# Value projections laid between the first maxima of attention, operands loaded during the adapter, and the last group's units exchanged

## The chip, the core and the metric

The program runs on one core of a Trainium2 chip. The core has five engines that run their own instruction lists and wait for each other with semaphores: TensorE (PE, matrix products; PEld is its loading of weights), VectorE (DVE), ScalarE (ACT), GpSimd (POOL) and SyncE (SP, which here only issues transfers). Matrix products go to PSUM, a memory of eight banks of 128 partitions x 512 floats; everything else lies in SBUF. The metric is the device time of one execution in microseconds; lower is better. One execution was also profiled, and all rows below come from it.

## What is computed

Two transformer layers in a row over 1024 tokens of 512 channels. The part that the change touches is the attention of both layers:

```python
# layer 0 (32 heads of 16 channels, causal), and an adapter of 10 prefix tokens
q, k, v = split(x @ w_attn.T); q, k = rope(q), rope(k)
y  = softmax(mask(q @ k.T / sqrt(16))) @ v
y += gating * softmax(q @ ak.T / sqrt(512)) @ av     # ak, av: projections of adapter_wte
x  = layernorm(x + y @ w_proj.T)
...
x  = layernorm(x + lookup(x))                        # memory lookup, not touched
# layer 1: 32 query heads share 8 key/value heads
q, k, v = x @ Wq, x @ Wk, x @ Wv; ... same attention, no adapter
x  = layernorm(x + y @ Wo)
x  = layernorm(x + swiglu(x))                        # not touched
```

## The kernel before, in words

`load_and_project` makes q and k of a layer in units of 128 channels x 512 tokens, rotates them, cuts each value into three bf16 parts that sum to it, and stores the parts in DRAM (`q_parts`, `k_parts`). Products with x and w are done as three fp32r products of cut operands (`products`, one output tile is 12 matmuls of 512 columns). In layer 1 this phase also makes the values v, as the last thing on PE: two tiles of 12 matmuls, copied by ACT into `v_T`, turned on PE in eight transposes and copied by ACT into `v_tok`.

`adapter` (layer 0 only) follows. Its list `order` sets what PE and ACT do: scores of four token tiles, then softmax of that half on DVE and ACT (`prob`), then for each of eight token tiles n a turn ("T": four transposes, ACT copies to `pT`) and a product ("y", ACT copies to `ad["y"]`). Between them stand eight tiles of the value projection ("V", 12 matmuls each, one ACT copy to `v_tok`). SP waits for the last V before it loads the first stacked operands of attention (`load_first`), because `arena_s`, where they go, also held the cut weights `w0_hl`.

`attention` works in units `(c, g)`: g is one of 8 groups of 4 heads, c one of 2 blocks of 512 query tokens. Unit c=0 is short (4 key tiles), c=1 long (8 key tiles). There are 16 units, c inside g. For each unit three things happen:

- *maxima*: bf16 products of q and k with a causal mask (lines 861 and 866), reduced by DVE (line 1001), joined by DVE (976), split by POOL (`split_max`, lines 1024 to 1030), turned on PE (entry "T", line 850), copied by DVE (992), and sent by an ACT-issued transfer into the rows under q (`load_max`, line 958). They run ahead of the unit by `LEAD` columns in three PSUM banks (`RING`).
- *scores* (line 886), exponentials on ACT (947), triangular masks on POOL for the diagonal tiles (1052).
- *values* (line 904), and one ACT copy of the unit's result (954, `copy_o`).

Before the first scores PE issues `maxima(0, 0)`: 48 entries, that is all maxima of units 0 and 1, the first of unit 2 and the turns of both units. This stretch is called the ramp below. `issued_by(u, slot)` tells how many entries PE has issued by a slot of unit u; POOL and ACT place their own work by it:

```python
while split < NU and min(first_entry[split + 1] + 3, first_entry[NU]) \
        <= issued_by(u, max(0, 2 * b - 4)):
    split_max(split)
```

ACT calls `load_max(u + 1)` at its fifth pair of exponentials of unit u. POOL starts the phase with three memsets (`k_st[KS:KM]`, line 1033) and `load_v(0)` (line 1010). Phases end with a barrier of all engines.

Of the kernel before, what the change touches and what calls it, by code (L numbers as in the profile page):

```python
# [26 lines left out]
F32 = mybir.dt.float32  # L27
# [80 lines left out]
def build(nc, d, out):  # L108
    with ExitStack() as stack:
# [5 lines left out]
        def at(name, offset, shape, dtype=F32):  # L115
# [22 lines left out]
        w0_hl = [at(f"w0_{n}", M_S + 24576 * n, [P, KC, 3 * C], F32R) for n in range(2)]  # L138
# [49 lines left out]
            w_hl=w0_hl, x_hl=x0_hl, q_parts=q_parts[0], k_parts=k_parts[0], ones=ones, eps=eps,  # L188
# [9 lines left out]
        adapter(nc, d, ad, x_loaded, x_tok, v_tok, w0_hl, x0_hl, arena_o, ident, gating, psum, stacked,  # L198
                wo[0], wo_hl[0])
        attention(nc, 0, att, stacked, arena_o, arena_p, arena_x, v_tok, v_grp, ident_b, maskb, psum,  # L200
                  (x_tok[:, :, :], d["x"].rearrange("(t p) c -> p t c", p=P), x_loaded))
# [15 lines left out]
        attention(nc, 1, att, stacked, arena_o, arena_p, arena_x, v_tok, v_grp, ident_b, maskb, psum)  # L217
# [45 lines left out]
def load_and_project(nc, d, layer, m):  # L263
# [8 lines left out]
    v_T = view(m["arena_w"], 0, [CH, 512])  # L272
# [28 lines left out]
    def cut_of(piece):  # L301

        kind, k, n0 = piece
        return [a[:, k, n0:n0 + 512] for a in ((x_raw, xh, xl) if kind == "x" else (w, wh, wl))]
# [8 lines left out]
    with Phase(nc, f"proj{layer}") as ph:  # L313
# [7 lines left out]
        v_ready, v_copied, consts = ph.sem("v_ready"), ph.sem("v_copied"), ph.sem("consts")  # L321
# [55 lines left out]
        def _(pe):  # L377
# [23 lines left out]
            if layer == 0:  # L401
# [12 lines left out]
                return  # L414

            for c in range(CH):
                products(pe, psum[:, 4 + c, :],
                         [lambda k, a=a: a[:, k, C + nk * P:n_out] for a in (wh, wl)],
                         [lambda k, a=a: a[:, k, 512 * c:512 * c + 512] for a in (xh, xl)])\
                    .then_inc(v_ready, 1)  # L420
            for c in range(CH):
                pe.wait_ge(v_copied, c + 1)
                for t in range(4):
                    last = pe.transpose(psum[:, 6 + c, P * t:P * t + P],
                                        v_T[:, c, P * t:P * t + P], m["ident"][:, :])
                last.then_inc(v_ready, 1)

        @block.scalar
        def _(act):
# [26 lines left out]
            for c in range(CH if layer == 1 else 0):  # L456
                act.wait_ge(v_ready, c + 1)
                act.copy(v_T[:, c, :], psum[:, 4 + c, :]).then_inc(v_copied, 1)
            for c in range(CH if layer == 1 else 0):
                act.wait_ge(v_ready, CH + c + 1)  # L460
                act.copy(v_tok[:, 4 * c:4 * c + 4, 0:P],
                         psum[:, 6 + c, :].rearrange("p (t f) -> p t f", f=P)).then_inc(v_copied, 1)
# [83 lines left out]
def adapter(nc, d, ad, x_loaded, x_tok, v_tok, w_hl, x_hl, arena_o, ident, gating, psum, stacked,  # L546
# [22 lines left out]
    turns = [what for what in order if what[0] in "VT"]  # L569
# [4 lines left out]
    with Phase(nc, "adapter") as ph:  # L574
# [19 lines left out]
        def _(pe):  # L594
            for what, n in order:
                if what == "scores":
# [22 lines left out]
                if what == "V":  # L619
                    last = products(pe, psum[:, bank, :],  # L620
                                    [lambda k, a=a: a[:, k, P * n:P * n + P] for a in x_hl],
                                    [lambda k, a=a: a[:, k, 2 * C:3 * C] for a in w_hl])
                else:
                    pe.wait_ge(prob_ready, n // HT + 1)
                    for t in range(KC):
                        last = pe.transpose(psum[0:AW, bank, P * t:P * t + P],
                                            prob[n // HT][:, n % HT, AW * t:AW * t + AW], ident[:, :])
# [3 lines left out]
        def _(act):  # L631
            for what, n in order:
# [3 lines left out]
                if what in "VT":  # L636
                    turn = turns.index((what, n))
                    bank = 4 + turn % 2
                    act.wait_ge(turn_ready, turn + 1)
                    if what == "V":  # L640
                        act.copy(v_tok[:, n, :], psum[:, bank, :]).then_inc(turn_taken, 1)
                    else:
                        if n >= 2:
                            act.wait_ge(y_ready, n - 1)
                        act.copy(pT[:, n % 2, :, :], psum[0:AW, bank, :].rearrange(
                            "p (t q) -> p t q", q=P)).then_inc(turn_taken, 1)
                if what == "V" and n in (0, 2):
                    half = n // 2
                    act.wait_ge(shifted, half + 1)
                    act.activation(prob[half], prob[half], ACT.Exp, scale=float(C) ** -0.5)\  # L650
                        .then_inc(exped, 1)
# [84 lines left out]
def attention(nc, layer, phase, stacked, arena_o, arena_p, arena_x, v_tok, v_grp, ident_b, maskb,  # L736
# [64 lines left out]
    with phase as ph, ExitStack() as own:  # L801
# [39 lines left out]
        def _(pe):  # L841
# [30 lines left out]
            def scores(u, kt, p):  # L872
# [4 lines left out]
                if kt == 0 and p == 0:  # L877
                    pe.wait_ge(max_loaded[u % NS], 16 * (u // NS + 1))
                    if u == 0:
                        pe.wait_ge(rows, NK)  # L880
# [936 lines left out]
```

## Time and profile before

| what | us |
|---|---|
| median of 3 runs (range) | 1014.57 (1011.73 to 1017.09) |
| the profiled execution: its time | 1011.6 |
| its span in the trace | 1009.9 |
| PE / DVE / ACT / POOL busy | 915.9 / 669.6 / 503.5 / 278.4 |
| adapter, from PE's first to the barrier behind it | 96.4 to 138.2 |
| ramp of layer 0, to its last turn | 138.3 to 165.1 |
| ramp of layer 1, to its last turn | 567.3 to 592.9 |

The span is what the trace covers; the 1.7 us between it and the time lie around the program and are taken as fixed. PE is the busiest engine by far, so the table is read by stages: in some of them PE sets the pace, in others it is paced by another.

### The profile page before, as it was taken

To read this page: it belongs to the slowest core of one execution; us is meant where nothing else is said; L and a number is where in the kernel's file an instruction comes from. 1 tells how busy PE (TensorE), PEld (TensorE's weight loads), DVE (VectorE), ACT (ScalarE), POOL (GpSimd) and SP (SyncE) were. 2 spreads that over 40 slices of the span, in tenths; PEclk is the share of its full clock that TensorE was granted. 3 is DMA by queue.
4 is the path that set the end of the run, shared out by engine and by line. 5 is a ranking of instruction groups with operands and counts; after the bars stand their busy time and mean duration, and the time that the engine had idled before them with its cause. 6 is when DMAs were issued, how large, how long until landed. Compare 5 with 4: busy or idle time off the path is not lost. (4 is left out here: it accounts for less than half of the span.)

```text
span 1009.9 us, 15158 instructions
## 1 busy us (share of the span) xinstructions
PE 915.9 (91%) x5334; PEld 503.2 (50%) x5334; DVE 669.6 (66%) x1177; ACT 503.5 (50%) x1134; POOL 278.4 (28%) x527
## 2 busy tenths in 40 slices
PE   6887989999999998988698599999999889799997
PEld 4555853433444432855365233434444338577766
DVE  5975547877788760965748577877778518455464
ACT  5221322776766665224612146777767652367630
POOL 2454141223223321033345122223223212013200
PEclk9997985999999999988789779999999999899999
DMA  9332060221212110200023400111100010321001
GB/s 323 94 95 79 1 149 25 55 53 54 65 49 63 47 40 7 99 1 1 0 75 112 111 22 25 37 40 39 41 26 2 2 42 1 136 82 64 22 32 53
DMA packets 50029, 57.14 MB, mean 57 GB/s; under 512 B 8928, under 2 KB 39712, under 8 KB 49952
## 3 DMA queue, kind: packets, MB, share of 16 engines
q1 hardware_dynamic: 48320, 55.75, 18.4%
q8 instruction: 45, 0.74, 0.3%
q10 hardware_dynamic: 1632, 0.39, 0.2%
q14 instruction: 32, 0.26, 0.1%
HBM read 43.41 MB, written 12.32 MB: 55 GB/s over the span
## 5 line engine op out<-in xcount | busy, mean ns | idle before, releaser
L1001 DVE TENSOR_REDUCE mx<-psum 128x1 f32<-128x512 f32 (+3 forms) x640 | 370.6, 631 | 114.5 <-PE psum L866 70.1
L861 PE MATMUL psum<-arena_s 96*128 96x512 bf16 (+3 forms) x768 | 226.5, 349 | 9.6 <-DVE mx L1001 5.5
L947 ACT ACTIVATE arena_p<-psum 128x512 f32<-128x512 f32 (+1 forms) x384 | 185.1, 591 | 92.7 <-PE psum L886 61.6
L886 PE MATMUL psum<-arena_s 99*128 99x512 bf16 (+3 forms) x768 | 204.4, 335 | 8.5 <-ACT arena_p L947 3.3
L947 ACT ACTIVATE arena_x<-psum 128x128 f32<-128x128 f32 (+2 forms) x384 | 133.9, 439 | 88.6 <-PE psum L886 65.7
L861 PEld LDWEIGHTS psum<-arena_s 96*128 96x128 bf16 x768 | 71.2, 99 | 124.4 <-DVE mx L1001 70.9
L886 PEld LDWEIGHTS psum<-arena_s 99*128 99x128 bf16 x768 | 66.9, 98 | 100.9 <-ACT arena_p L947 34.4
L1052 POOL TENSOR_SCALAR_AFFINE_SELECT arena_p<-arena_p 128x256 f32<-128x256 f32 x128 | 50.9, 408 | 204.2 <-ACT arena_p L947 204.2
L259 PE MATMUL psum<-x_h,w 128*128 128x512 f32 x224 | 87.9, 456 | 10.8 <-DVE w L476 7.6
L866 PE MATMUL psum<-maskb,ident_b 128*128 128x128 bf16 (+1 forms) x384 | 96.5, 251 | 0.0
L904 PE MATMUL psum<-arena_p,v_grp 128*32 128x512 f32 (+1 forms) x768 | 91.5, 597 | 0.0
L1052 POOL TENSOR_SCALAR_AFFINE_SELECT arena_x<-arena_x 128x256 f32<-128x256 f32 x128 | 51.4, 408 | 76.9 <-ACT arena_x L947 47.2
L904 PE MATMUL psum<-arena_x,v_grp 128*32 128x256 f32 (+2 forms) x768 | 59.0, 421 | 4.6 <-POOL arena_x L1052 4.6
L434 ACT CAST arena_p<-arena_o 128x512 bf16<-128x512 f32 x26 | 16.1, 619 | 87.3 <-DMA q_parts<-arena_p 42.7
L259 PEld LDWEIGHTS psum<-x_h,w 128*128 128x128 f32 x224 | 44.8, 200 | 27.5 <-DVE w L476 9.2
L1603 PE MATMUL psum<-x_h,ff_w 128*128 128x512 f32 (+1 forms) x176 | 45.7, 403 | 1.6 <-ACT ff_flags L1660 0.9
L468 DVE CAST arena_p<-arena_o 128x512 bf16<-128x512 f32 x26 | 32.2, 1240 | 21.6 <-POOL arena_o L542 21.5
L259 PE MATMUL psum<-x_l,w 128*128 128x512 f32 x112 | 46.2, 413 | 0.0
L1603 PE MATMUL psum<-x_l,ff_w 128*128 128x512 f32 (+1 forms) x176 | 45.2, 399 | 0.0
L1140 PE MATMUL psum<-wo_h,yT 128*128 128x512 f32 x128 | 43.8, 403 | 1.6 <-DVE arena_s L1213 1.6
L542 POOL TENSOR_TENSOR arena_o<-arena_o,arena_p 128x512 f32<-128x512 f32 x26 | 31.7, 1220 | 46.5 <-ACT arena_p L434 46.5
L538 POOL TENSOR_TENSOR arena_o<-arena_o 128x512 f32<-128x512 f32 x26 | 34.3, 1319 | 33.2 <-DVE arena_o L494 33.2
(202 smaller groups left out, 1203.6 us busy)
## 6 DMA issues: line engine op xcount, KB each, us to landing
q_parts<-arena_p SPq DMA_DIRECT2D x48, 128.0 KB
arena_s<-q_parts SPq DMA_DIRECT2D x32, 192.0 KB, 2.9
arena_s<-k_parts SPq DMA_DIRECT2D x96, 64.0 KB, 2.3
ff_raw<-in_w_in SPq DMA_DIRECT2D x11, 512.0 KB, 3.6
arena_s<-q_parts SPq DMA_DIRECT2D x32, 128.0 KB, 3.0
k_parts<-arena_p SPq DMA_DIRECT2D x30, 128.0 KB
arena_w<-in_w SPq DMA_DIRECT2D x12, 256.0 KB, 6.5
ff_wd_raw<-in_w_down SPq DMA_DIRECT2D x1, 2560.0 KB, 11.3
```

The source lines that it names most:

```text
L259: last = pe.matmul(out, lhs[i](k), rhs[j](k), start=k + n == 0, stop=k == KC - 1 and n == 2)
L468: dve.tensor_copy(parts[:, n % 2, 1, :], t_cos[:, n % 2, :]).then_inc(mid_ready, 1)
L538: pool.tensor_tensor(rotated(n), t_cos[:, s, :], t_sin[:, s, :], ALU.add)\
L861: last = pe.matmul(psum[:, bank, width * n:width * n + width], q_st[0:KS, b % NS, 512 * r + P * i:512 * r + P * i + P], k_st[0:KS, g % NK, ...
L866: last = pe.matmul(psum[:, bank, 0:width * n].rearrange("p (h k) -> p h k", h=n) [:, :, width - P:width], ident_b[:, :], maskb[:, :].rearr ...
L886: pe.matmul(psum[:, 2 * (n % 2) + t, o:512], k_st[0:KM, g % NK, at:at + P], q_st[0:KM, u % NS, 512 * r + o:512 * r + 512], start=True, sto ...
L904: last = pe.matmul(psum[32 * r:32 * r + VW, 6, o:512], v_grp[:, u // CH % 2, kt, r if layer == 0 else 0, :], pr[(n + r // 2) % NP_RING][:, ...
L947: act.activation(pr[n % NP_RING][:, t, o:512], psum[:, 2 * (n % 2) + t, o:512], ACT.Exp, scale=scale).then_inc(exp_ready, 1)
L1001: dve.tensor_reduce(mx[:, b % 2, kc, col:col + 4 * len(heads) - 3:4], src, AX, ALU.max)\
L1052: pool.affine_select(out=tri, in_=tri, compare_op=ALU.is_ge, fill=0.0, base=0, pattern=[[0, 2], [1, P]], channel_multiplier=-1).then_inc(m ...
L1140: last = pe.matmul(psum[:, 5, :], yT_hl[i][:, t % 2, k, :], w_out[j][:, k, :], start=k + n == 0, stop=k == KC - 1 and n == 2)
L1603: last = pe.matmul(psum[0:rows[i], 2 * (n % 3) + u, :], ff.w_hl[a][:, i % 2, col:col + rows[i]], x_hl[b][:, k, 512 * c:512 * c + 512], sta ...
```

## The change

Five edits. (1) In layer 0 the 96 value matmuls leave the adapter, in layer 1 the 24 value matmuls and eight transposes leave the projection phase; both are laid between the entries of the ramp (`v_product`, `v_turn`): by entry e of 48, e/42 of them are issued. ACT's copies of them come at the head of its list in attention. (2) The cut weights of v get arrays of their own (`wv0_hl`) at the end of the old ones, so SP issues `load_first` at the adapter's start; the loads whose place they still hold wait for the last v product. (3) POOL's memsets write 2048 floats instead of 4096 bf16, and the third one and `load_v(0)` come after the splits of units 0 and 1. (4) ACT's `load_max` is placed by `issued_by`, and slots below zero now reach back into the unit before. (5) The last two units are exchanged: (1, 7), then (0, 7).

```diff
+UNITS = [(c, g) for g in range(NG - 1) for c in range(CH)] + [(1, NG - 1), (0, NG - 1)]
...
-    order = [("scores", 0), ("V", 0), ("V", 1), ("scores", 1)]
-    for n in range(NT):
-        order.append(("T", n))
-        if n < 3:
-            order += [("V", 2 * n + 2), ("V", 2 * n + 3), ("y", n)]
-        elif n > 3:
-            order.append(("y", n - 1))
+    order = [("scores", 0), ("scores", 1)]
+    for n in range(NT):
+        order.append(("T", n))
+        if n == 2:
+            order.append(("exp", 1))
+        if n:
+            order.append(("y", n - 1))
...
-            sp.wait_ge(turn_ready, turns.index(("V", NT - 1)) + 1)
             stacked.load_first(sp)
...
+            if layer == 0:
+                stacked.load_q(sp, 3)
+            sp.wait_ge(v_ready, V_DONE)
+            if layer == 1:
+                stacked.load_q(sp, 3)
             stacked.load_q(sp, 4)
...
+                    if u == 0:
+                        pe.wait_ge(v_copied, V_COPIED)
...
-            maxima(0, 0)
+            ramp = issued_by(0, 0)
+            n_products = 3 * KC * V_DONE
+            for e in range(ramp):
+                b = next(x for x in range(NU + 1) if issued < first_entry[x + 1])
+                entry(issued, b, lists[b][issued - first_entry[b]])
+                issued += 1
+                done = min(n_products, n_products * e // (ramp - 6))
+                for i in range(done, min(n_products, n_products * (e + 1) // (ramp - 6))):
+                    v_product(i)
+                if layer == 1 and e in (ramp - 4, ramp - 1):
+                    v_turn(0 if e == ramp - 4 else 1)
...
-            load_max(0)
+            for t in range(V_DONE):
+                act.wait_ge(v_ready, t + 1)
...
+                if t == V_DONE // 2:
+                    load_max(0)
+            sent = 1
             for u in range(NU):
                 for b in range(2 * n_tiles[steps[u][0]]):
+                    while sent < NU and turn_entry(sent) < issued_by(u, 2 * b - 6):
+                        load_max(sent)
+                        sent += 1
                     exp(u, b)
                     if u and b == 3:
                         copy_o(u - 1)
-                    if u + 1 < NU and b == 4:
-                        load_max(u + 1)
```

PE's list at the start of layer 0's ramp (`arena_s` holds the stacked q and k, `maskb` the mask; line 861 before is line 847 after, 866 is 852), before:

```order
L861 MATMUL psum<-arena_s 128x128 [waits att0_k_loaded00,att0_q_loaded0]
L861 MATMUL psum<-arena_s 128x128
L866 MATMUL psum<-maskb,ident_b 128x256
L861 MATMUL psum<-arena_s 128x128 x2
L866 MATMUL psum<-maskb,ident_b 128x256
```

and after, where `wv_0` and `wv_1` are the cut weights of v and `x_h`, `x_l` the cut tokens:

```order
L847 MATMUL psum<-arena_s 128x128 [waits att0_k_loaded00,att0_q_loaded0]
L847 MATMUL psum<-arena_s 128x128
L852 MATMUL psum<-maskb,ident_b 128x256
L919 MATMUL psum<-wv_0_65,x_h 128x512
L919 MATMUL psum<-wv_1_66,x_h 128x512
L847 MATMUL psum<-arena_s 128x128 x2
L852 MATMUL psum<-maskb,ident_b 128x256
L919 MATMUL psum<-wv_0_65,x_l 128x512
L919 MATMUL psum<-wv_0_65,x_h 128x512
```

Behind each of the first 42 entries two or three value matmuls of 512 columns now stand.

ACT's list at the start of attention in layer 1 (`mT` is the turned maxima, `arena_w` holds `v_T`), before:

```order
L958 DMA arena_s<-mT 3x16x128 [waits att1_qk_taken]
L947 ACT_TABLE_LOAD
L947 ACTIVATE arena_p<-psum 128x512 [waits att1_scores_ready] x4
L947 ACTIVATE arena_p<-psum 128x384 [waits att1_scores_ready] x4
L947 ACTIVATE arena_x<-psum 128x256 [waits att1_scores_ready] x2
L958 DMA arena_s<-mT 3x16x128 [waits att1_qk_taken]
```

and after:

```order
L988 COPY arena_w<-psum 128x512 [waits att1_v_ready] x2
L980 DMA arena_s<-mT 3x16x128 [waits att1_qk_taken]
L994 COPY v_tok<-psum 128x4x128 [waits att1_v_ready] x2
L980 DMA arena_s<-mT 3x16x128 [waits att1_qk_taken]
L969 ACT_TABLE_LOAD
L969 ACTIVATE arena_p<-psum 128x512 [waits att1_scores_ready] x4
```

The second copy of turned values, the second transfer of maxima and the load of the exponential's table now stand ahead of the first exponential.

PE's list at the end of layer 1's ramp, after (line 835 is the turn of the maxima, 927 the turn of the values, 874 the scores):

```order
L847 MATMUL psum<-arena_s 128x384 [waits att1_qk_taken]
L852 MATMUL psum<-maskb,ident_b 128x128
L835 MATMUL psum<-ident_b,mst 48x128 [waits att1_max_ready,att1_qk_taken]
L927 MATMUL psum<-ident,arena_w 128x128 [waits att1_v_copied]
L927 MATMUL psum<-ident,arena_w 128x128 x3
L874 MATMUL psum<-arena_s 128x512 [waits att1_rows,att1_v_copied,att1_max_loaded0]
```

Before, the scores followed the turn of the maxima directly; now four transposes and a wait for ACT's last copy stand between.

## Rows read from the trace of the kernel before

**Rows 1.** The page's first part: busy time, share, instructions

```profile
PE 915.9 (91%) x5334; PEld 503.2 (50%) x5334; DVE 669.6 (66%) x1177; ACT 503.5 (50%) x1134; POOL 278.4 (28%) x527
```

**Rows 2.** Stretches: length, engines' busy time (PE, PEld, DVE, ACT, POOL), clock, DMA

```profile
78.00:82.00 4.00, 0.97 (x3) 0.30 (x2) 3.45 (x4) 1.10 (x2) 2.22 (x3) 1.00 0.30 96
82.00:93.00 11.00, 11.00 (x39) 8.08 (x38) 6.74 (x8) 1.24 (x2) 5.12 (x5) 0.53 0.33 106
96.40:138.30 41.90, 40.48 (x256) 35.98 (x256) 14.40 (x12) 15.68 (x26) 7.55 (x9) 1.00 0.15 37
138.30:165.10 26.80, 23.23 (x90) 7.81 (x90) 24.39 (x47) 0.00 (x0) 12.48 (x12) 0.61 0.35 84
165.10:174.90 9.80, 9.80 (x41) 3.21 (x41) 3.35 (x7) 5.15 (x14) 2.84 (x7) 0.50 0.22 62
200.00:350.00 150.00, 147.69 (x1124) 61.15 (x1121) 120.47 (x223) 104.68 (x259) 44.74 (x130) 1.00 0.21 55
545.00:549.00 4.00, 0.97 (x3) 0.19 (x2) 3.42 (x4) 1.10 (x2) 2.22 (x3) 1.00 0.29 96
567.30:592.90 25.60, 23.62 (x89) 8.43 (x89) 24.48 (x47) 1.28 (x1) 4.62 (x12) 0.63 0.25 67
```

**Rows 3.** Timeline of the adapter, DVE and ACT: start, length, engine, line

```profile
100.27 1.49 DVE L663 TENSOR_REDUCE arena_f<-psum 128x128 f32<-128x1280 f32 x1 [4.43 <-PE psum L602]
...
113.23 1.28 ACT L650 ACTIVATE arena_o<-arena_o 128x1280 f32<-128x1280 f32 x1
...
117.37 1.49 DVE L671 TENSOR_TENSOR arena_o<-arena_o,arena_f 128x1280 f32<-128x1280 f32 x1
...
130.50 1.07 ACT L645 COPY arena_o<-psum 80x512 f32<-80x512 f32 x2
...
137.30 0.59 ACT L635 COPY arena_w<-psum 128x512 f32<-128x512 f32 x1 [0.40 <-PE psum L611]
```

**Rows 4.** Timeline of PE: first matmul of value tile 1, first after it

```profile
102.88 0.61 PE L259 MATMUL psum<-w,x_h 128*128 128x512 f32 x2
...
105.60 0.56 PE L602 MATMUL psum<-arena_f,arena_o 128*128 128x80 f32 x4
```

**Rows 5.** Timeline of layer 0's ramp, POOL and PE

```profile
138.16 10.41 POOL L1033 MEMSET arena_s<- 3x4096 bf16 x3 [33.99 <-POOLq L244]
...
150.38 0.27 PE L850 MATMUL psum<-ident_b,mst 128*48 128x128 bf16 x1 [2.03 <-POOL mst L1030]
...
165.05 0.30 PE L850 MATMUL psum<-ident_b,mst 128*48 128x128 bf16 x1
```

**Rows 6.** Timeline of PE: from bf16 to fp32 operands

```profile
210.96 0.38 PE L861 MATMUL psum<-arena_s 96*128 96x512 bf16 x1
...
211.27 1.92 PE L904 MATMUL psum<-arena_p,v_grp 128*32 128x512 f32 x16
```

**Rows 7.** Timeline of ACT: first exponentials and first result copy, both layers

```profile
165.93 3.60 ACT L947 ACTIVATE arena_p<-psum 128x512 f32<-128x512 f32 x8 [28.04 <-DVE mx L1001]
...
179.87 0.59 ACT L954 COPY arena_o<-psum 128x512 f32<-128x512 f32 x1
...
593.82 3.60 ACT L947 ACTIVATE arena_p<-psum 128x512 f32<-128x512 f32 x8 [12.66 <-PE psum L886]
...
605.40 0.59 ACT L954 COPY arena_o<-psum 128x512 f32<-128x512 f32 x1
```

**Rows 8.** Timeline of layer 1: table load, last turn, sending of maxima

```profile
579.88 1.28 ACT L947 ACT_TABLE_LOAD   x1 [14.56 <-DVE mx L1001]
...
592.94 0.30 PE L850 MATMUL psum<-ident_b,mst 128*48 128x128 bf16 x1
...
597.03 0.73 ACTq L958 DMA_DIRECT2D arena_s<-mT  x1
```

**Rows 9.** Timeline of SP: last stores of layer 1's projection phase

```profile
556.29 10.19 SPq L363 DMA_DIRECT2D q_parts<-arena_p  x9
```

**Rows 10.** Timeline of ACT in layer 0's last short unit

```profile
381.39 0.45 ACT L947 ACTIVATE arena_x<-psum 128x128 f32<-128x128 f32 x2 [2.91 <-PE psum L886]
```

More of the change, by code:

```diff
@@ L595, in _ @@
             for what, n in order:
+                if what == "exp":
+                    continue
                 if what == "scores":
@@ L618, in _ @@
                 bank = 4 + turn % 2
[L619 to L627, printed above, removed]
+                pe.wait_ge(prob_ready, n // HT + 1)
+                for t in range(KC):
+                    last = pe.transpose(psum[0:AW, bank, P * t:P * t + P],
+                                        prob[n // HT][:, n % HT, AW * t:AW * t + AW], ident[:, :])
                 last.then_inc(turn_ready, 1)
@@ L635, in _ @@
                     act.copy(y_ad[:, n, :], psum[:, 6 + n % 2, :]).then_inc(y_copied, 1)
[L636 to L650, printed above, removed]
+                if what == "T":
+                    act.wait_ge(turn_ready, n + 1)
+                    if n >= 2:
+                        act.wait_ge(y_ready, n - 1)
+                    act.copy(pT[:, n % 2, :, :], psum[0:AW, 4 + n % 2, :].rearrange(
+                        "p (t q) -> p t q", q=P)).then_inc(turn_taken, 1)
+                if (what, n) in (("scores", 0), ("exp", 1)):
+                    act.wait_ge(shifted, n + 1)
+                    act.activation(prob[n], prob[n], ACT.Exp, scale=float(C) ** -0.5)\
                         .then_inc(exped, 1)
@@ L749, in attention @@
     n_tiles = [4 * (c + 1) for c in range(CH)]
-    steps = [(c, g) for g in range(NG) for c in range(CH)]
+    steps = UNITS
     NU = len(steps)
@@ L787, in issued_by @@
     def issued_by(u, slot):
-        done = sum(unit_columns[0:u]) + unit_columns[u] * slot // (4 * n_tiles[steps[u][0]])
+        if slot < 0 and u > 0:
+            return issued_by(u - 1, slot + 4 * n_tiles[steps[u - 1][0]])
+        done = sum(unit_columns[0:u]) + unit_columns[u] * max(0, slot) // (4 * n_tiles[steps[u][0]])
         return sum(1 for n in reached if n <= done + LEAD)
@@ L917, in maxima, with v_product, v_turn @@
                     issued += 1
-            maxima(0, 0)
+            def v_product(i):
+                tile, step = divmod(i, 3 * KC)
+                k, n = divmod(step, 3)
+                a, b = ((0, 0), (0, 1), (1, 0))[n]
+                xs, ws = v_from["x"], v_from["w"]
+                if layer == 0:
+                    bank, lhs, rhs = tile % 4, xs[a][:, k, P * tile:P * tile + P], ws[b][:, k, :]
+                    if step == 0 and tile >= 4:
+                        pe.wait_ge(v_copied, tile - 3)
+                else:
+                    bank, lhs, rhs = tile, ws[a][:, k, C + P:C + 2 * P], xs[b][:, k, 512 * tile:512 * tile + 512]
+                last = pe.matmul(psum[:, bank, :], lhs, rhs, start=step == 0, stop=step == 3 * KC - 1)
+                if step == 3 * KC - 1:
+                    last.then_inc(v_ready, 1)
+            def v_turn(c):
+                pe.wait_ge(v_copied, c + 1)
+                for t in range(4):
+                    last = pe.transpose(psum[:, 2 + c, P * t:P * t + P],
+                                        v_from["v_T"][:, c, P * t:P * t + P], v_from["ident"][:, :])
+                last.then_inc(v_ready, 1)
+            ramp = issued_by(0, 0)
[9 more added lines that the diff above has]
+                    v_turn(0 if e == ramp - 4 else 1)
             for u, kt in blocks[0:2]:
@@ L1030, in split_max, with minus @@
                 pool.tensor_tensor(low, md[:, :], mid, ALU.subtract).then_inc(max_ready, 1)
-            for s in range(NK):
-                pool.memset(k_st[KS:KM, s, :], -1.0).then_inc(rows, 1)
-            pool.wait_ge(rows, NK)
-            load_v(0)
+            two_minus = float(np.uint32(0xBF80BF80).view(np.float32))
+            def minus(slot):
+                pool.memset(k_st[KS:KM, slot, :].bitcast(F32), two_minus).then_inc(rows, 1)
+                pool.wait_ge(rows, slot + 1)
+            minus(0)
+            minus(1)
             split = 0
```

81 lines of the change are left out of this document (42 added, 39 removed).

## The prediction

> **What bounds the kernel now.** I read the page's first part, then a table of stretches, then the timelines of the places that the change touches. PE is busy for 91% of the span [rows 1], so the first question is where it isn't the engine that sets the pace. The stretches say so [rows 2]. In the middle of attention (200 to 350) PE is busy 147.7 of 150 us at a clock of 1.00 (2.4 GHz): work moved there would only lengthen it. In the adapter (96.4 to 138.3) PE is busy 40.5 of 41.9 us, but about half of that is the value projection. In the ramp of layer 0 (138.3 to 165.1) DVE is busy 24.4 of 26.8 us, and PE's 23.2 us of busy time stand at a clock of 0.61: it streams few columns and is paced by DVE. The ramp of layer 1 is the same picture, DVE 24.5 of 25.6 us. So the change takes work from a stretch that PE bounds and gives it to one that DVE bounds. What counts is whether the receiver has room.
>
> **Adapter, layer 0.** Without V, what is left is a chain of DVE and ACT and its tail. DVE starts on the first scores at 100.27 and ends the second half's softmax at 117.37 + 1.49 = 118.86 [rows 3]. V hardly delayed that chain: ACT's second exponential (113.23) stood behind a copy of a value tile, and by my walk through the new order it comes 0.5 us sooner, so the softmax ends at 118.4. Then four rounds of turn and product follow. In the old trace the last five turns' copies start with the pair at 130.50 (its second, the first of the second half, at 130.50 + 1.07 - 0.58 = 131.0), and the last copy ends at 137.30 + 0.59 = 137.9 [rows 3]: 6.9 us. With the same tail behind a first copy at 119.1 the adapter ends at 126.0, **-11.9 us**. V's own 96 matmuls would be more: tile 1 takes 105.60 - 102.88 = 2.72 us for 12, or 0.227 us each [rows 4], 21.8 us in all; some 10 us of it was already behind the softmax.
>
> **Loads during the adapter.** SP now issues the first operands at 96.4. The ramp's first matmul came with the barrier, before too; nothing waited for them: **0**. They are hidden by the softmax, and would cost at most the few us that they take to issue if that cover were gone. The loads that must wait for the last v product (third k slot, fifth q slot) are used a group later, over 20 us on.
>
> **Ramp, layer 0.** The maxima of the 48 entries are 20,736 columns of scores and 5,376 of mask (5,120 in the short unit 0, 13,312 in the long unit 1, 2,304 of unit 2; 128 columns of mask for each of 42 diagonal tiles): 26,112 columns, 10.9 us at 2.4 GHz, and with 14 ns for the start of each of some 90 instructions (what 0.227 us has over 512 columns) 12.1 us. V adds 21.8 us. That is 33.9 us of PE against DVE's 24.4: **PE becomes the bound of the ramp**. To this comes a change of operands from bf16 to fp32r and back behind each of 42 entries, which no trace of before shows. The nearest row is the step from maxima to values: a 512-column matmul starts at 210.96, the next at 211.27 [rows 6], 0.31 us where 0.22 would do, so up to 0.1 us one way. Bounds: nothing, and 0.2 us for there and back (8.4 us); I take 0.08 us, 3.4 us, nearer to the row's one way, since the trace's values also use a narrow column position. Last, the turn of unit 1 waits for DVE and POOL some 0.3 us. Together 37.5 us against 165.05 - 138.3 = 26.8 [rows 5]: **+10.7 us**. PE's wait of 2.03 us for POOL behind 10.41 us of memsets [rows 5] goes too, but it was DVE's slack and is inside this difference.
>
> The Trainium skill (TensorE: Matmul & The Clock Gate, LDWEIGHTS) has a load of weights take its columns over 1.2 GHz, which for 128 columns is an estimated 107 ns, about 53 ns more than the 128-column mask ahead of it covers. By that rule the 42 changes would cost at most 2.3 us, and the whole sum below would be about 1 us less; no run here shows it.
>
> **First exponentials, layer 0.** ACT now sends the maxima of unit 1 before its first exponential. It waits for DVE's copy of the last turn and then issues for 0.73 us [rows 8]: an estimated **+0.9 us**. Against it stands the clock: from 165.1 to 174.9 PE ran at 0.50 [rows 2]. From first exponential to first result copy layer 0 took 179.87 - 165.93 = 13.9 us, layer 1, mostly at 2.4 GHz, 605.40 - 593.82 = 11.6 us [rows 7]. A ramp full of products should leave the clock high: **-2.4 us**. `load_v(0)` and the third memset (about 0.6 and, by half of 3.47 us a memset, 1.8 us) are covered by ACT's first pair of exponentials.
>
> **Layer 1.** The end of the projection phase is set by SP: nine stores issued from 556.29 for 10.19 us, to 566.48 [rows 9], less than 1 us before the ramp. They wait for the parts of the last two units, not for PE's value products. Taking these away gives **0**. In the ramp 24 products (5.5 us) and eight transposes (some 1.1 us: four of them are at most 0.6 of a round's 1.4 us in the adapter's tail, 6.9 us over five) join 12.1 us of maxima: 19 us, within DVE's 24.5, so they are hidden at 2.4 GHz. At 1.2 GHz, as in much of this ramp (clock 0.63 in rows 2), they aren't: each entry with its half product then takes PE 860 columns or 0.72 us against DVE's 24.4 / 46 = 0.53, until the clock comes back. For some seven entries that is **+1.3 us** (bounds 0 and, at 1.2 GHz throughout, 8). The end of the ramp is surer. Before, the last turn was at 592.94 and the first exponential at 593.82, 0.9 us [rows 7, 8]. Now four transposes (0.6 us with the start), ACT's copy (0.6), the issue of the second maxima (0.73) and the table load of 1.28 us, which had been done idle at 579.88 [rows 8], stand in line: 3.6 us, **+2.8 us** (bounds 2 and 3.5).
>
> **The exchanged units.** The tail without maxima has the same columns either way. PE's wait for POOL's last mask ahead of unit 14 stays, since POOL still splits the last maxima ahead of that mask, and DVE is done with them no sooner. The wait of ACT for 2.91 us came with a low clock [rows 10]. I take **0**, bounds -4 and +2 a layer. The new places of `load_max` and of the splits move nothing that PE waited for in the middle: **0**.
>
> **The clock in the adapter.** Without V, PE idles in it three times: about 3 us while DVE takes the first scores, 2 us, and 3.9 us ahead of the fifth turn. Two similar stretches with PE busy 0.97 of 4 us stand in rows 2: after 78 to 82 the clock was 0.53 for 11 us, in 545 to 549 it stayed 1.00. At 1.2 GHz a round of the tail takes PE about 2.9 us instead of 1.4, over four rounds 6 us. I take half: **+3.0 us**.
>
> **Sum.** -11.9 + 3.0 + 10.7 + 0.9 - 2.4 + 1.3 + 2.8 = **+4.4 us**. The profiled execution took 1011.6 us (span 1009.9 and 1.7 around it), so it would take 1016.0. The median of the runs lies 3.0 above it; against that the forecast is 1014.6 + 4.4 = **1019.0 us**, +0.4%. About 0.5% (5 us) is what a measurement of this kernel can tell from no change.
>
> **The rivals.**
> - *The clock falls early and stays down (slower).* If PE is at 1.2 GHz from the first gap to the start of the ramp, the second scores take 3.7 us more, the tail 6 instead of 3, and the ramp, now bound by PE, loses 2.5 us or more until the clock is back; with as much again in layer 1's ramp the sum is about +14, 1028 us. It decides from 1 us of extra low time on the PE-bound part. For it: after 82 the clock stayed low for 11 us of busy PE. Against it: the second gap in rows 2. The Trainium skill (TensorE: Matmul & The Clock Gate, Why this matters for your kernels) tells to leave no long idle gaps between bursts, since the clock then falls to half; it speaks for this rival, and the trace agrees once and disagrees once. Chance 0.25.
> - *The tail gains and the gaps are harmless (faster).* If the long unit ahead of the short one keeps PE fed, its low clock and ACT's wait of 2.91 us go, about 4 us in layer 0 and 3 in layer 1. With a full clock in the adapter (-3) the sum is about -5.5, 1009 us. Against it: the wait for the mask, which begins it, stays. Chance 0.16.
> - *The change does what it says: V is hidden in DVE's ramp.* Then the ramp stays 26.8 us and the sum is -6.3, 1008 us. Against it stand 75,000 columns, 31 us at 2.4 GHz, in a ramp of 27. Only a wrong count of mine would allow it. Chance 0.09.
> - *Forecast.* Chance 0.50, own range 1014 to 1024.
>
> **How the numbers follow.** The range of 0.8 runs from the faster cases (1008) to the better part of the slow one (1027). Faster by over 0.5% (under 1009.5) holds most of the two faster cases, 0.19. Slower (over 1019.6) holds nearly all of the slow clock and 0.16 of the forecast, 0.40. Within 0.5%: 0.41.
>
> **What the new profile would show.** The adapter should be 29 to 33 us long with PE's clock below 1 in its last third; the ramp of layer 0 37 to 38 us with PE busy throughout at clock 1.00, DVE waiting between reductions, and no wait for the memset; the first exponential of layer 1 about 3.6 us behind the last turn, with the table load right ahead of it; layer 1's projection phase still ending with some 10 us of stores on SP; both tails 29 to 31 us. A ramp of layer 0 under 34 us, or a tail under 27, would make me wrong to the fast side; a ramp over 40 us, or a clock of 0.5 in it, to the slow side.

## The result, and the profile after

The changed kernel takes 1061.26 us (median of 4 runs, 1059.92 to 1063.06) against 1014.21 us for the kernel before: a ratio of 1.046, 95% interval 1.043 to 1.050. It is 47 us slower; the prediction said 4.4 us slower, with a range up to 1027.

The first thing to do with a miss of this size is to find the stretch. ACT copies each unit's result once, so its copies (line 954 before, 976 after) are milestones in both traces. From the starts of the first and the last copy of each layer:

| stretch | before, us | after, us | difference | the prediction's sum |
|---|---|---|---|---|
| to the first copy of layer 0 | 179.87 | 184.29 | +4.4 | +0.3 |
| first to last copy, layer 0 | 220.02 | 237.63 | +17.6 | 0 |
| to the first copy of layer 1 | 205.51 | 209.68 | +4.2 | +4.1 |
| first to last copy, layer 1 | 221.54 | 241.72 | +20.2 | 0 |
| to the end of the span | 182.94 | 184.88 | +1.9 | 0 |

So 37.8 of the 48.3 us by which the span grew were lost in the middle of attention, where the prediction had put nothing. The first part of the profile's page has PE's share down from 91% [rows 1] to 88%, with the same number of matmuls in it:

```profile
PE 929.9 (88%) x5334; PEld 510.8 (48%) x5334; DVE 672.7 (64%) x1177; ACT 502.8 (48%) x1134; POOL 272.9 (26%) x527
```

The view of stretches shows where (columns: stretch, its length, busy time of PE, PEld, DVE, ACT and POOL, PE's clock, DMA):

```profile
core 0: us, PE busy (x) PEld busy (x) DVE busy (x) ACT busy (x) POOL busy (x), PEclk, DMA share, GB/s
200.00:350.00 150.00, 138.31 (x1014) 55.68 (x1012) 108.17 (x200) 94.00 (x231) 39.69 (x118) 0.98 0.20 52
```

PE was busy for 147.7 of these 150 us before [rows 2]; now it stands for 11.7. The groups of PE's lines in the same stretch name what it waits for (line 874 is the scores):

```profile
L847 PE MATMUL psum<-arena_s 96*128 96x512 bf16 (+3 forms) x222 | 60.8, 327 | 1.0 <-DVE mx L1036 1.0
L874 PE MATMUL psum<-arena_s 99*128 99x512 bf16 (+3 forms) x222 | 59.2, 330 | 10.6 <-ACT arena_p L969 8.4 <-ACT arena_x L969 1.3
```

The scores wait 10.6 us, nearly all for ACT's exponentials to free a bank. Why is ACT late, when it has over 50 us of idle time in this stretch? Its timeline at one short unit (line 969 exponentials, 976 the copy, 980 the transfer of the maxima):

```profile
231.65 2.83 ACT L969 ACTIVATE arena_p<-psum 128x512 f32<-128x512 f32 x6 [0.38 <-PE psum L874]
237.38 0.73 ACTq L980 DMA_DIRECT2D arena_s<-mT  x1
238.21 0.87 ACT L969 ACTIVATE arena_p<-psum 128x384 f32<-128x384 f32 x2 [3.73 <-DVE mx L1036]
238.96 0.59 ACT L976 COPY arena_o<-psum 128x512 f32<-128x512 f32 x1
239.43 1.59 ACT L969 ACTIVATE arena_x<-psum 128x256 f32<-128x256 f32 x6
244.47 0.45 ACT L969 ACTIVATE arena_x<-psum 128x128 f32<-128x128 f32 x2 [3.46 <-PE psum L874]
```

ACT ends its exponentials at 234.48 and then does nothing for 2.9 us: the next instruction in its list is the transfer of the next unit's maxima, which needs DVE's copy of the turn. The timelines of PE and DVE show where that copy comes from, and what PE does meanwhile (line 835 is the turn, 1027 DVE's copy of it, 892 the values):

```profile
236.35 0.24 PE L835 MATMUL psum<-ident_b,mst 128*48 128x128 bf16 x1
236.52 0.39 PE L874 MATMUL psum<-arena_s 99*128 99x256 bf16 x2
...
238.75 0.67 PE L874 MATMUL psum<-arena_s 99*128 99x256 bf16 x2 [1.54 <-ACT arena_p L969]
...
239.90 0.51 PE L874 MATMUL psum<-arena_s 99*128 99x128 bf16 x2 [0.26 <-ACT arena_x L969]
...
241.00 3.21 PE L892 MATMUL psum<-arena_p,v_grp 128*32 128x512 f32 x16
```

```profile
235.60 1.62 DVE L1036 TENSOR_REDUCE mx<-psum 128x2 f32<-128x512 f32 x3 [0.48 <-PE psum L852]
237.14 0.20 DVE L1027 COPY mT<-psum 48x128 bf16<-48x128 bf16 x1
```

PE turns the maxima at 236.35 and DVE, behind three reductions, copies them at 237.14. Only then does ACT get past its transfer, and the exponentials of pair 3, for which PE is standing, start at 238.21. PE loses 1.54 and 0.26 us. Then something more: the 16 value matmuls at 241.00 take 3.21 us. The stretches give the reason, here and at the same place one group earlier:

```profile
205.00:209.50 4.50, 2.52 (x18) 1.00 (x20) 2.12 (x6) 2.81 (x9) 1.18 (x4) 1.00 0.27 69
209.50:213.00 3.50, 3.50 (x29) 1.25 (x22) 2.36 (x5) 1.65 (x5) 1.37 (x5) 1.00 0.10 30
237.00:241.00 4.00, 2.05 (x13) 0.73 (x11) 1.65 (x5) 2.79 (x9) 1.07 (x3) 0.96 0.25 66
241.00:244.20 3.20, 3.20 (x18) 0.65 (x18) 1.01 (x2) 0.01 (x1) 0.51 (x2) 0.51 0.13 38
```

Behind the gap in 237 to 241 the granted clock is at its lower level (0.51, 1.2 GHz) for 3.2 us; behind the same gap at 205 it isn't, and 16 such matmuls take 1.71 us there. The copies account for nearly all of it. In layer 0 the copies of a short and a long unit are 23.0 us apart where it was 20.64 (179.87 to 200.51), in each of the first five groups, and the next copy follows after 10.2 us where it was 8.59, in two of these groups: 5 x 2.4 + 2 x 1.6 = 15.2 us of the 17.6.

Why is the transfer there? The prediction read the rule `turn_entry(sent) < issued_by(u, 2 * b - 6)` as leaving it in place. In a long unit that is so: it comes behind pair 4, as before. In a short unit the turn stands at the end of the unit ahead, so slot 0 already satisfies the rule, and slot 0 is b = 3. The transfer moved from behind pair 4 to ahead of pair 3.

### The profile page after: what moved, and what is told of

Same layout as the page of the kernel before. It is cut to its first block and busy times, and to the rows that moved or that the text cites. A ratio compares the mean times of both kernels' runs of the same rounds, so it can differ in the third digit from the quotient of the medians.

```text
span 1058.2 us, 15178 instructions
## 1 busy us (share of the span) xinstructions
PE 929.9 (88%) x5334; PEld 510.8 (48%) x5334; DVE 672.7 (64%) x1177; ACT 502.8 (48%) x1134; POOL 272.9 (26%) x527
## 5 line engine op out<-in xcount | busy, mean ns | idle before, releaser
L1036 DVE TENSOR_REDUCE mx<-psum 128x1 f32<-128x512 f32 (+3 forms) x640 | 374.4, 631 | 155.8 <-PE psum L852 107.3
L847 PE MATMUL psum<-arena_s 96*128 96x512 bf16 (+3 forms) x768 | 220.1, 336 | 22.1 <-PEq L246 17.6
L969 ACT ACTIVATE arena_x<-psum 128x512 f32<-128x512 f32 (+2 forms) x384 | 132.8, 448 | 103.2 <-PE psum L874 73.1
L892 PE MATMUL psum<-arena_p,v_grp 128*32 128x512 f32 (+1 forms) x768 | 99.6, 643 | 0.0
L852 PE MATMUL psum<-maskb,ident_b 128*128 128x128 bf16 (+1 forms) x384 | 93.7, 244 | 0.0
L261 PE MATMUL psum<-x_h,w 128*128 128x512 f32 x208 | 82.4, 459 | 11.0 <-DVE w L459 7.9
L892 PE MATMUL psum<-arena_x,v_grp 128*32 128x512 f32 (+2 forms) x768 | 59.1, 421 | 3.7 <-POOL arena_x L1098 3.7
L261 PEld LDWEIGHTS psum<-x_h,w 128*128 128x128 f32 x208 | 41.8, 201 | 26.8 <-DVE w L459 9.4
L892 PEld LDWEIGHTS psum<-arena_p,v_grp 128*32 128x32 f32 x768 | 21.8, 119 | 50.3 <-issue 31.6
L261 PE MATMUL psum<-x_l,w 128*128 128x512 f32 x104 | 43.0, 413 | 0.0
```

The source lines that it names most:

```text
L261: last = pe.matmul(out, lhs[i](k), rhs[j](k), start=k + n == 0, stop=k == KC - 1 and n == 2)
L847: last = pe.matmul(psum[:, bank, width * n:width * n + width], q_st[0:KS, b % NS, 512 * r + P * i:512 * r + P * i + P], k_st[0:KS, g % NK, ...
L852: last = pe.matmul(psum[:, bank, 0:width * n].rearrange("p (h k) -> p h k", h=n) [:, :, width - P:width], ident_b[:, :], maskb[:, :].rearr ...
L892: last = pe.matmul(psum[32 * r:32 * r + VW, 6, o:512], v_grp[:, steps[u][1] % 2, kt, r if layer == 0 else 0, :], pr[(n + r // 2) % NP_RING ...
L969: act.activation(pr[n % NP_RING][:, t, o:512], psum[:, 2 * (n % 2) + t, o:512], ACT.Exp, scale=scale).then_inc(exp_ready, 1)
L1036: dve.tensor_reduce(mx[:, b % 2, kc, col:col + 4 * len(heads) - 3:4], src, AX, ALU.max)\
```

## The experiments

**One number of the rule.** Three kernels and one more, on one chip (before: 1014.45 us). The first (`...` marks what a cut of code leaves out, here and below):

```
-  while sent < NU and turn_entry(sent) < issued_by(u, 2 * b - 6):
+  while sent < NU and turn_entry(sent) < issued_by(u, 2 * b - 8):
```

> The changed kernel, with one number other: ACT sends the maxima of a unit once the turn stands at least 8 slots back instead of 6, that is one pair of exponentials later. Main theory (ACT's sending of the maxima was moved ahead of the pair b = 3 of each short unit, where it waits for DVE's copy): the steady group takes 29.2 us again instead of 31.6 and 33.2, which takes back most of the 17.6 us in the middle of layer 0 and of the 20.2 us of layer 1, and the time is about 1023 us (1019 to 1028). Rival 1 (the place of POOL's splits costs it): no change, 1061. Rival 2 (the waits for the halves of k, or the phase in which the value products leave PE): no change, 1061.

Measured: 1032.2 us (1.018, 1.014 to 1.022). 29 of the 47 us are back, but not the 38 that the main theory wanted, and both rivals, which expected no change, fall. ACT's timeline of this kernel at the same unit tells what is left:

```profile
233.21 0.87 ACT L969 ACTIVATE arena_p<-psum 128x384 f32<-128x384 f32 x2 [1.35 <-PE psum L874]
233.96 0.59 ACT L976 COPY arena_o<-psum 128x512 f32<-128x512 f32 x1
234.76 0.73 ACTq L980 DMA_DIRECT2D arena_s<-mT  x1
235.59 1.55 ACT L969 ACTIVATE arena_x<-psum 128x256 f32<-128x256 f32 x6 [1.03 <-DVE mx L1036]
```

"One pair later" is ahead of pair 4, and the place of before was behind it. The transfer still stands 1.03 us in front of the exponentials, PE waits 0.97 us for them, and a group takes 30.07 us where it took 29.23.

**The splits alone.**

```
   ...                                    # POOL, split_max
-  <= issued_by(u, 2 * b - 4):
+  <= issued_by(u, max(0, 2 * b - 4)):
```

> The changed kernel with POOL's splits where they stood before (their slot held at 0 or more), ACT's sends as changed. Main theory (ACT's place of the send): no change, 1061 us within 3. Rival (the later splits make the turn on PE late): about 1023 us.

Measured: 1064.3 us (1.047, 1.043 to 1.050), 3.1 us above the changed kernel, with overlapping intervals. Putting POOL's splits back gives nothing back; their place is no part of the 47 us.

**The new rule in the kernel before.**

```
+  if slot < 0 and u > 0: ...             # issued_by, as in the changed kernel
...
+  while sent < NU and turn_entry(sent) < issued_by(u, 2 * b - 6):
+      load_max(sent); sent += 1
   exp(u, b)
   if u and b == 3: copy_o(u - 1)
-  if u + 1 < NU and b == 4: load_max(u + 1)
```

> The kernel before, with only the rule for ACT's sends of the changed kernel (turn at least 6 slots back, instead of a fixed place behind pair 4). Main theory: 2.4 us of every group, 14 groups, 34 us, and with the clock's fall in every second group about 1.6 us more, 10 us: 1014 + 35 to 45, about 1055 us. Rival (the loss needs the value products in the ramp, the exchanged units or the splits): 1014 us within 3.

Measured: 1068.8 us (1.053, 1.048 to 1.058). The rule alone costs 54 us, more than in the changed kernel; value products, exchanged units and splits aren't needed for it. 50.7 us of them lie between the first and last copies of the two layers. Its timeline has the same wait at the same place:

```profile
236.30 0.73 ACTq L960 DMA_DIRECT2D arena_s<-mT  x1
237.13 0.87 ACT L949 ACTIVATE arena_p<-psum 128x384 f32<-128x384 f32 x2 [3.73 <-DVE mx L1005]
```

The expected 35 to 45 us were too few because the clock fell more often:

```profile
200.00:350.00 150.00, 140.17 (x959) 55.03 (x959) 101.72 (x187) 87.24 (x218) 39.09 (x117) 0.90 0.19 49
```

0.90 over these 150 us, where the changed kernel has 0.98.

The same rule also sends unit 1's maxima ahead of the first exponential, and this trace shows what that costs. In layer 1 PE's last turn starts at 624.73, and ACT has

```profile
625.76 0.73 ACTq L960 DMA_DIRECT2D arena_s<-mT  x1
626.52 1.28 ACT L949 ACT_TABLE_LOAD   x1 [29.56 <-DVE mT L996]
```

with the first exponential at 627.81, 3.1 us behind the turn; the kernel before had 0.9. No value product lies in this kernel's ramp. The section on why the prediction was wrong comes back to it.

**Two pairs later.** (Before, in this set: 1015.2 us.)

```
-  while sent < NU and turn_entry(sent) < issued_by(u, 2 * b - 6):
+  while sent < NU and turn_entry(sent) < issued_by(u, 2 * b - 10):
```

> The changed kernel with ACT's send two pairs later than changed (turn at least 10 slots back), which in a short unit puts it behind pair 4, where it stood before. Main theory (the place of the send on ACT is the whole loss of the middle): the run one pair later still had 1 us of wait ahead of pair 4 and groups of 30.1 us, since it put the send ahead of pair 4 and not behind it; now the group takes 29.2 us as before and PE's wait in front of the third tile of scores is gone. 14 times 0.84 and some 3 to 5 us of low clock come back: 1032.2 - 12 - 3 = 1017 us (1014 to 1021). Rival (a second loss is left in the middle, from the splits or the waits for k): 1028 to 1033 us.

Measured: 1016.3 us (1.002, 1.000 to 1.004), as the main theory says. ACT's timeline:

```profile
230.59 0.87 ACT L969 ACTIVATE arena_p<-psum 128x384 f32<-128x384 f32 x2 [1.35 <-PE psum L874]
231.34 0.59 ACT L976 COPY arena_o<-psum 128x512 f32<-128x512 f32 x1
231.81 0.69 ACT L969 ACTIVATE arena_x<-psum 128x256 f32<-128x256 f32 x2
232.14 0.73 ACTq L980 DMA_DIRECT2D arena_s<-mT  x1
232.97 1.00 ACT L969 ACTIVATE arena_x<-psum 128x256 f32<-128x256 f32 x4 [0.47 <-PE psum L874]
```

The transfer is issued without a wait while PE has work. PE is busy for 148.67 of the 150 us from 200 to 350, 1.0 more than before. The three places give a measured curve: behind pair 4 nothing that can be told from before, ahead of pair 4 about 16 us, ahead of pair 3 about 45 us.

The number moves the transfer in a long unit too: ahead of pair 5 in the changed kernel, of 6 and of 7 in these two runs. In the kernel before ACT waits 1.63 us around this transfer in a long unit,

```profile
212.31 1.08 ACT L947 ACTIVATE arena_x<-psum 128x512 f32<-128x512 f32 x2 [1.63 <-DVE mx L1001]
```

and PE then waits 0.15 us for ACT's exponentials; with the transfer two pairs later neither wait is left, and the copies of a short and a long unit are 20.33 us apart instead of 20.64. No run changes the place in long units alone, so this cause is argued and not shown. Between first and last copies the two layers together take 438.9 us, against 441.6 before.

**The exchanged units.** The kernel with the send one pair later, and

```
-UNITS = [... for g in range(NG - 1) ...] + [(1, NG - 1), (0, NG - 1)]
+UNITS = [(c, g) for g in range(NG) for c in range(CH)]
```

> The changed kernel with the send one pair later, and the last two units in their old order (short, then long). Main theory of the exchanged units: they are worth nothing that can be told, so this is within 3 us of the kernel with the later send alone. Rival: the exchange gains about 3.5 us a layer in the tails, so this is about 7 us slower than that one. Second rival: the exchange itself costs, since the last sends then have other places; this is up to 5 us faster.

Measured: 1037.9 us (1.023, 1.019 to 1.027), 5.7 us slower than with the exchange. That was the first rival's sign, but it can't be read as the exchange's worth: the traces differ by 3.1 us before the first copy (186.65 against 183.55), where both kernels are the same. A second pair was run with the send two pairs later and half of V in the adapter (below):

> As the kernel with half of V of layer 0 in the adapter, with the last two units in their old order. Main theory (the exchange is worth nothing that can be told, as in the tails read so far: layer 0 73.6 to 76.0 us against 73.8, layer 1 72.2 to 74.3 against 75.0): 1003.3 within 2. Rival (it gains, by the pair with the send one pair later, 1032.2 against 1037.9): 1006 to 1009 us.

Measured: 1002.2 us (0.985, 0.983 to 0.988), against 1003.3 (0.989, 0.985 to 0.993) with the exchange, on another chip. Nothing can be told between them. The first pair's difference stays unexplained.

**Where V is worth most.** All from here have the send two pairs later. The value products of layer 1 back at the end of the projection phase:

```
+  for c in range(CH):                    # load_and_project, layer 1, as before
+      products(pe, psum[:, 4 + c, :], ...).then_inc(v_ready, 1)
-  V_DONE = NT if layer == 0 else CH      # attention
+  V_DONE = NT if layer == 0 else 0
```

> As the kernel with the send two pairs later, and the value products of layer 1 back in the projection phase, those of layer 0 still in the ramp. Main theory, by the terms of the prediction for layer 1 (1.3 for the clock in the ramp, 2.8 for the chain behind its last turn): 4 us faster than with the send two later. Rival: the projection phase or the chain hides them alike, within 1 us.

Measured: 1018.4 us (1.005, 1.001 to 1.008; single runs from 1013.5 to 1025.9), against 1016.3. The expected 4 us can't be seen. In the profiled runs the stretch between the layers is 208.1 us against 211.7, so it may be there under a spread of 12 us; the medians don't show it. Of the expected 4 us, 2.8 were for the chain behind the last turn, and this trace has that chain unchanged without value products in the ramp: last turn at 593.42, first exponential at 596.50. And all eight tiles of layer 0 back in the adapter, layer 1 in the ramp:

```
-  order = [("scores", 0), ("scores", 1)] ...
+  order = [("scores", 0), ("V", 0), ("exp", 0), ("V", 1), ("scores", 1)] ...   # as before
```

> As the kernel with the send two pairs later, and all eight value tiles of layer 0 back in the adapter, those of layer 1 still in the ramp. The traces of the changed kernels show the first result copy of layer 0 at 182.5 to 186.7 us, before at 179.9: main theory 3 to 4 us faster than with the send two later. Rival (the stretch up to there swings with the clock of the run and the place of V is worth nothing): within 1 us.

Measured: 1013.0 us (0.998, 0.996 to 1.001): 3.3 us faster than with V in the ramp, as expected (10 runs of each, whose ranges overlap), and the same as before.

**Half of V in each.** Neither place is right for all of it: the adapter has gaps, and the ramp has room under DVE, for about half. The value products of layer 1 are in the projection phase here, and stay there in all kernels below.

```
+  order = [("scores", 0), ("V", 0), ("exp", 0), ("V", 1), ("scores", 1)]
+  for n in range(NT):
+      order.append(("T", n))
+      if n == 0: order += [("V", 2), ("exp", 1), ("V", 3)]
+      if n: order.append(("y", n - 1))
...
+  V_FIRST, V_DONE = 4, 4                 # attention, layer 0: tiles 4 to 7 in the ramp
```

> Send two pairs later; value tiles 0 to 3 of layer 0 in the adapter, in the gaps in which PE waits for the softmax, tiles 4 to 7 in the ramp; the value products of layer 1 in the projection phase. Main theory (each stretch has room for half): the adapter takes 32 instead of 41.9 us, since 10.9 us of products lie in gaps of 3.1 and 4.1 us and keep the clock up; the ramp holds 12.1 + 10.9 us of PE under DVE's 26.8 and stays at 27 to 28 us. That is 9 to 10 us under the kernel before: 1002 to 1007 us. Rival (the changes of operands and the clock take it back): 1010 to 1015 us.

Measured: 1003.3 us (0.989, 0.985 to 0.993). Adapter and ramp of this kernel:

```profile
98.00:128.20 30.20, 29.08 (x208) 26.75 (x209) 14.41 (x12) 13.32 (x22) 7.43 (x9) 1.00 0.21 53
128.20:153.90 25.70, 25.21 (x138) 13.59 (x138) 24.61 (x47) 2.34 (x4) 5.56 (x11) 1.00 0.28 73
```

against the changed kernel's

```profile
96.40:132.00 35.60, 26.54 (x160) 25.39 (x160) 14.84 (x13) 11.26 (x18) 7.33 (x8) 0.76 0.17 45
132.00:168.60 36.60, 35.97 (x186) 21.01 (x186) 27.91 (x47) 4.69 (x8) 6.10 (x12) 1.00 0.21 52
```

With half of V each stretch is full: PE 29.1 of 30.2 us at a clock of 1.00 in the adapter, DVE 24.6 of 25.7 in the ramp, with PE busy under it. From PE's first scores of the adapter to the last turn of the ramp it is 97.86 to 153.75, 55.9 us; in the changed kernel 97.39 to 168.55, 71.2 us; before 96.46 to 165.05 [rows 5], 68.6 us.

**The first transfer behind the first exponentials.**

```
-  while sent < NU and turn_entry(sent) < issued_by(u, 2 * b - 10):
+  while sent < NU and u + b // 2 and turn_entry(sent) < issued_by(u, 2 * b - 10):
```

> As the kernel with half of V of layer 0 in the adapter, and the maxima of unit 1 sent behind the first pair of exponentials instead of ahead of the first. The trace with V of layer 1 in the projection shows ACT's table load of 1.28 us and the send of 0.73 us in line between the last turn and the first exponential (596.50), where the kernel before had the table load done in the idle time. Main theory: 2 us in layer 1 and 0.8 us in layer 0 come back, 1003.3 - 2.8 = 1000.5 us (999 to 1002). Rival (the first exponentials aren't what the stretch ends on): 1003 us within 1.

The code puts the transfer behind the first two pairs, b = 0 and 1. Measured: 1000.4 us (0.982, 0.979 to 0.985; before 1017.9 in this set). The time is the one that was expected, but 1003.3 was measured on another chip, and in this set the kernel with the old order of units, which sends ahead of the first exponential, took 1002.2; so the medians alone don't settle it. The traces do. ACT's timeline in layer 1 shows the table load back in the idle time:

```profile
571.53 0.76 ACTq L1016 DMA_DIRECT2D arena_s<-mT  x1
572.32 1.28 ACT L1005 ACT_TABLE_LOAD   x1 [14.57 <-DVE mx L1074]
586.27 1.57 ACT L1005 ACTIVATE arena_p<-psum 128x512 f32<-128x512 f32 x3 [12.66 <-PE psum L910]
587.35 0.73 ACTq L1016 DMA_DIRECT2D arena_s<-mT  x1
```

The last turn of this ramp is at 585.39, so the first exponential comes 0.9 us behind it, where it was 3.1; in layer 0 it is 0.6 instead of 1.8. That is 3.4 us in both layers, and the first copy of layer 1 follows after 11.6 us instead of 13.3.

Last, the adapter's second exponential ahead of the copy of tile 2 (`[("exp", 1), ("V", 2), ("V", 3)]`):

> As the kernel with the first send behind the exponentials, and ACT's second exponential of the adapter ahead of the copy of value tile 2. In the trace of the kernel with half of V it became ready at 113.74 and started at 114.62, behind that copy. Main theory: 0.9 us sooner through the whole softmax, 999.6 us. Rival (DVE or PE's products hold the end of the softmax): no difference to the kernel with the first send behind the exponentials.

Measured: 995.9 us (0.980, 0.975 to 0.984; single runs from 991.9 to 1005.5). Against the trace of the kernel with half of V the exponential starts at 113.92 instead of 114.62, but the last copy of the adapter comes 29.3 us behind PE's first scores in both: the rival holds as far as the adapter goes, and the edit gave nothing there. So the 4.6 us between the medians aren't its work. The clock can make such a difference with the same instructions in place: from 101 to 109 the profiled run of the kernel ahead has a granted clock of 0.50, where this one and the one with half of V have 1.00, and the first copy of V in its adapter comes 5 us later (the first row is the kernel ahead, the second this one):

```profile
101.00:109.00 8.00, 8.00 (x28) 7.03 (x28) 2.98 (x2) 0.00 (x0) 4.62 (x5) 0.50 0.58 142
101.00:109.00 8.00, 8.00 (x49) 7.02 (x48) 5.50 (x5) 2.35 (x3) 4.53 (x5) 1.00 0.62 142
```

This is the fastest version by its median; its runs spread over 14 us, its interval overlaps that of the one ahead of it, and it isn't shown to be faster.

## Why the prediction was wrong

**The step that failed** reads: "The new places of `load_max` and of the splits move nothing that PE waited for in the middle: **0**." For the splits it holds (1064.3 with them put back, 1061.3 without). For `load_max` it cost the changed kernel 1061.3 - 1016.3 = 45 us. What was wrong is not a duration but a place that was never worked out: the rule was checked for where the turn is issued, not for which b of a short unit first satisfies it. The order lists of ACT show it without any time: ahead of the change a result copy is followed by two exponentials and then the transfer; in the changed kernel's short units the transfer comes two exponentials ahead of the copy. The question that the prediction should have asked at this line is its own one for added waits: what is queued behind the waiting instruction on its engine (pair 3), and who waits for that (PE, for a bank). No rival had it either: all three moved the time by the clock, the tail or the ramp.

With that one step undone the kernel takes 1016.3 us (ratio 1.002); the sum of the other terms was +4.4, 1019.0. That agreement is partly luck: the middle came out 2.7 us shorter than before, where the sum had nothing, and the terms in the changed kernel's own trace came out like this:

- **Adapter, -11.9 and +3.0 for the clock.** From PE's first scores to the barrier it took 97.39 to 132.04, 34.7 us, against 96.46 to 138.16, 41.7: -7.0, where the two terms make -8.9 (another 0.9 us were lost ahead of it, in the projection phase, which the change didn't mean to touch). The clock took more back than the half that was allowed: it is 0.76 on average in the row above, and the second half's scores took 7.1 us instead of 3.7. The rival of the low clock was right here and wrong behind it, since the ramp ran at 1.00 throughout.
- **Ramp of layer 0, +10.7.** 36.5 us from barrier to last turn against 26.9: +9.6. PE did become the bound (35.97 of 36.6 us). The sum was 37.5; that by the Trainium skill (TensorE: Matmul & The Clock Gate, LDWEIGHTS) was about 1 us less, and the total in this trace agrees with it. No run has the changes of operands by themselves, so their share stays an estimate.
- **First exponentials, +0.9** came out: 1.8 us behind the last turn instead of 0.9. **The clock after it, -2.4**, did not: 13.94 us to the first copy, as before. PE waits 1.25 us for ACT's first exponentials, and behind that the clock is at 0.50 from 174 to 178. The full ramp didn't carry the clock past this wait.
- **Layer 1, +1.3 and +2.8.** The ramp cost nothing: its products lay under DVE (23.9 of 24.7 us). The chain behind it was 3.1 us instead of 0.9, +2.2, but not by all the parts that were named. The kernel with the new send alone, and those with V of layer 1 in the projection phase and the send still ahead of the first exponential, have the same 3.1 us without a transpose or a copy of values in the ramp: it is DVE's copy of the turn with the transfer behind it (1.8 us, as in layer 0) and the table load (1.28). The value transposes and their copy, for which the sum had 1.2 us, lie beside it and cost nothing. So this term belongs to the rule for `load_max`, and not to the value products. Another 2.3 us came between the first exponential and the first copy, 13.8 instead of 11.6 (14.1 in the kernel with the new send alone), and it is the clock again: 0.50 from 622 to 626, where in the kernel before it was at 1.00 from 598 on (both rows below, the kernel before first). The sum of 4.1 was met (4.2) by other terms.

```profile
598.00:602.00 4.00, 4.00 (x33) 1.65 (x33) 2.85 (x5) 2.05 (x8) 1.59 (x4) 1.00 0.08 26
622.00:626.00 4.00, 4.00 (x24) 1.33 (x22) 1.92 (x4) 0.91 (x4) 1.20 (x3) 0.50 0.07 25
```

- **The loads, 0**: held; no wait of PE for a transfer shows in the adapter or in the ramp of layer 0.
- **The exchanged units, 0**: not contradicted; one pair of runs says 5.7 us in their favour, the other nothing. The tail of layer 0 (from the copy that starts at 345.70) is 76.2 us against 73.8, that of layer 1 75.1 against 75.0.
- **The last 1.9 us**, behind attention, also come and go between the experiments (183.2 to 185.0 us from last copy to end); nothing in the change was found that makes them.

## What to carry to other kernels

A transfer that waits is as expensive as what stands behind it in its engine's list. When a rule such as "so many slots behind" replaces a fixed place, work out for each kind of unit at which step it first fires and compare the engine's list there, row by row; a shift by one pair of exponentials was worth 29 us in this kernel, the next one 16. An engine with much idle time (ACT, 94 of 150 us busy) can still be the one that the bound engine waits for. And before moving all of a block of work from one stretch to another, ask how much each can hide: here half and half gave 1003 us, where all in the adapter gave 1013 (with V of layer 1 in its ramp) and all in the ramp 1016 to 1018 (with V of layer 1 in either place).

## What the runs showed of the hardware

In the changed kernel a wait of PE of 1.54 us, with one of 0.26 behind it, was followed by a fall of the granted clock from 1.00 to 0.51 (2.4 to 1.2 GHz) for 3.2 us, which cost 1.6 us more; in layer 0 only at every second such wait, though the work around it was the same (205 and 237 us above). With the same wait in the kernel before, the copies of layer 0 show such a fall in each of the first five groups (a spacing of 10.2 to 11.2 us instead of 8.59). With the send one pair later, where the wait is a single one of 1.0 us, it fell behind one of the first five:

```profile
268.00:270.00 2.00, 2.00 (x16) 0.39 (x8) 0.43 (x1) 0.00 (x0) 0.00 (x0) 0.52 0.00 0
```

With the send two pairs later neither the waits nor the falls are there. What decides at which wait the clock falls no run here shows. The Trainium skill (TensorE: Matmul & The Clock Gate, Why this matters for your kernels) warns of idle gaps longer than the sum of the first two; the traces show falls behind shorter ones than that section names, and the measurement decides.
